# Twelve-layer decoder on one core: the eight stack-building DMAs of each 16-head self attention move from SyncE's queue to ScalarE's

## The reference, cut to what matters

```python
def heads(W):
    return (x @ W).reshape(B, S, NUM_HEADS, D_K).transpose(0, 2, 1, 3)   # 16 heads, D_K = 8
Q, K, V = (heads(WQ), heads(WK), heads(WV))
score = jnp.einsum('bhqd,bhkd->bhqk', Q, K) / jnp.sqrt(jnp.asarray(D_K, x.dtype))
score = score + mask                                   # causal
score = score - jnp.max(score, axis=-1, keepdims=True)
score = jnp.exp(score)
score = score / jnp.sum(score, axis=-1, keepdims=True)
out = jnp.einsum('bhqk,bhkd->bhqd', score, V)
```

## Time and profile before

| | |
|---|---|
| median of 3 runs | 3130.19 us (3121.03 to 3132.73) |
| the profiled execution | 3134.6 us, span 3132.9 us |
| granted TensorE clock, mean | 0.849 |
| PE busy | 2589.2 us, 83% |
| DVE busy | 1766.1 us, 56% |
| ACT busy | 1299.1 us, 41% |
| POOL busy | 635.5 us, 20% |
| DMAs `stacks<-parts` | 96 of 256 KB |

### The profile page before, as it was taken

The page is one execution under the profiler, slowest core; times in us unless marked ns, Lnnn a source line. Parts: engine busy times, 40 slices in busy tenths (PEclk is TensorE's granted clock), DMA queues, the critical chain, the costliest instruction groups (busy, mean ns, idle before and its releaser), DMA issues.

```text
span 3132.9 us, 38544 instructions
## 1 busy us (share of the span) xinstructions
PE 2589.2 (83%) x13201; PEld 1302.8 (42%) x13201; DVE 1766.1 (56%) x4879; ACT 1299.1 (41%) x3060; POOL 635.5 (20%) x893
## 2 busy tenths in 40 slices
PE   5788898789987887887758988987899888878865
PEld 2233335334544685224323333452345447742243
DVE  5544437645654688625455544486356448876164
ACT  1555621452323542574324556214532344434741
POOL 1320001320112583000113100013201137720000
PEclk7899897788877998888759988987798789988886
DMA  5100002200100001200210000022001000021000
GB/s 179 29 1 1 1 1 53 54 2 21 34 14 1 1 28 34 49 1 31 65 27 10 1 1 1 1 53 53 2 21 34 14 1 1 29 54 28 1 1 7
DMA packets 42054, 73.34 MB, mean 23 GB/s; under 512 B 2881, under 2 KB 34689, under 8 KB 40066
## 3 DMA queue, kind: packets, MB, share of 16 engines
q1 hardware_dynamic: 41282, 69.58, 8.7%
q10 hardware_dynamic: 576, 1.29, 0.1%
HBM read 43.86 MB, written 1.05 MB: 14 GB/s over the span
## 4 chain that ended last, share of the span: by engine, by line
PE 61%; DVE 18%; ACT 10%; issue 7%; DMA 2%; POOL 2%; ACTq 0%; DVEq 0%; POOLq 0%; SPq 0%
PE psum L564 4%; PE psum L986 4%; PE psum L2159 4%; PE psum L997 3%; DVE floor_s L2258 3%; PE psum L554 3%; ACT PT_s L1018 2%; PE psum L1534 2%; PE psum L810 2%; PE psum L1364 2%; PE psum L735 2%; ACT PT_s L630 2%; PE psum L1826 2%; DVE mx_s L699 2%; PE psum L537 2%
## 5 line engine op out<-in xcount | busy, mean ns | idle before, releaser
L630 ACT ACTIVATE PT_s<-psum 128x512 f32<-128x512 f32 (+3 forms) x768 | 342.5, 499 | 249.5 <-PE psum L554 247.8
L386 POOL TENSOR_SCALAR ve<-mv 128x4 f32<-128x4 f32 x48 | 13.5, 282 | 1609.1 <-DVE mv L376 1608.9
L2185 POOL TENSOR_TENSOR buffer<-sim_s 128x1024 f32<-128x1024 f32 x128 | 270.7, 2130 | 165.0 <-DVE floor_s L2258 86.9
L537 PE MATMUL psum<-stacks_s 64*128 64x512 bf16 (+3 forms) x768 | 210.7, 402 | 100.9 <-DMA stacks_s<-parts_s 39.7
L696 DVE CUSTOM_DVE_ANT_0 rest_s<-psum,packed_early 128x128 f32<-128x128 f32 (+3 forms) x512 | 225.1, 488 | 71.7 <-PE psum L537 69.2
L564 PE MATMUL psum<-PT_s,vaug 128*9 128x512 f32 (+3 forms) x1536 | 183.5, 554 | 57.3 <-POOL PT_s L669 40.1
L554 PE MATMUL psum<-stacks_s 64*128 64x512 bf16 (+3 forms) x768 | 194.5, 369 | 38.1 <-ACT PT_s L630 24.0
L669 POOL TENSOR_SCALAR_AFFINE_SELECT PT_s<-PT_s 128x128 f32<-128x128 f32 x512 | 148.1, 300 | 359.5 <-ACT PT_s L630 355.1
L2218 ACT ACTIVATE above_s<-buffer,below_s 128x1024 f32<-128x1024 f32 x128 | 145.7, 1151 | 132.2 <-PE psum L2159 88.3
L1036 ACT ACTIVATE PT_s<-psum 128x512 f32<-128x512 f32 (+1 forms) x224 | 121.2, 593 | 167.9 <-PE psum L988 167.8
L699 DVE TENSOR_REDUCE mx_s<-psum 128x1 f32<-128x512 f32 x256 | 160.1, 686 | 44.3 <-PE psum L537 43.5
(11 more groups left out here) (448 smaller groups left out, 5074.6 us busy)
## 6 DMA issues: line engine op xcount, KB each, us to landing
stacks_s<-parts_s SPq DMA_DIRECT2D x96, 256.0 KB, 5.6
buffer<-packed_experts SPq DMA_DIRECT2D x36, 384.0 KB, 3.5
buffer<-packed_moe SPq DMA_DIRECT2D x4, 2048.0 KB, 8.3
buffer<-packed_cross SPq DMA_DIRECT2D x4, 2048.0 KB, 7.5
buffer<-packed_product SPq DMA_DIRECT2D x4, 1024.0 KB, 4.7
packed_early<-packed_early SPq DMA_DIRECT2D x1, 2654.0 KB
raw_s<-packed_setup SPq DMA_DIRECT2D x1, 1840.0 KB, 6.9
packed_late<-packed_late ACTq DMA_DIRECT2D x4, 314.0 KB, 3.8
```

The lines of the kernel that those rows point to most:

```text
L537: pe.matmul(bank[n % 4][:, 0:n_keys], QS[half(h), h // 2, j * P:(j + 1) * P], KS[half(h), h // 2, 0:n_keys], start=True, stop=True, tile_p ...
L630: a.activation(PT[:, u // 4 % 2, i, q0_of(c):T], bank[u % 3][:, q0_of(c):T], ACT.Exp, scale=scale).then_inc(exp_done.sem, 1)
L2185: g.tensor_tensor(fs[:, n % 2], m[:, 0, :].unsqueeze(2).to_broadcast([P, NK, NK]), m[:, 1, :].unsqueeze(1).to_broadcast([P, NK, NK]), ALU. ...
```

## The change

The waits and the eight DMAs leave SyncE's generator and stand in ScalarE's, behind its four copies of the parts, at the same planned time `T1 - 2`. Tiles, transfers, semaphores and everything on TensorE, VectorE and GpSimd stay as they are.

```diff
     def sync(sp):
-        yield T1 - 2
-        for ready in (keys_split(4), queries_split(4), keys_repeated(2), queries_repeated(2), pads_set(3)):
-            sp.wait_ge(*ready)
-        for loaded, (first, last) in zip(pairs_loaded, PAIR_GROUPS):
-            for i in range(first, last):
-                sp.dma_start(stacks[:, :, i, :], parts[2 * HD8 * i:2 * HD8 * (i + 1)]).then_inc(loaded.sem, 16)
         for t, kind, u in plan:
             yield t
             if kind == "spread":
@@ def scalar(a): behind the four copies of the parts
                 a.copy(to, parts[:, FIRST_SLOT[name][n]:FIRST_SLOT[name][n] + 1, q, :].to_broadcast(to.shape)).then_inc(repeated.sem, 1)
+        yield T1 - 2
+        for ready in (keys_split(4), queries_split(4), keys_repeated(2), queries_repeated(2), pads_set(3)):
+            a.wait_ge(*ready)
+        for loaded, (first, last) in zip(pairs_loaded, PAIR_GROUPS):
+            for i in range(first, last):
+                a.dma_start(stacks[:, :, i, :], parts[2 * HD8 * i:2 * HD8 * (i + 1)]).then_inc(loaded.sem, 16)
         for t, kind, u in plan:
             yield t
             if kind == "rows":
```

## The result

The changed kernel is slower: median 3215.07 us (3213.81 to 3222.24, 4 runs) against 3128.11 us (3121.03 to 3132.73, 4 runs), ratio 1.0278, 95% interval 1.0260 to 1.0296, which is +87 us. Measured again on another chip, beside nine more runs of the kernel before, it was 1.0265 (1.0251 to 1.0279), +83 us. The forecast was 3210 us, +80. The profiled execution has a span of 3220.5 us where the one before had 3132.9.

The account below looks back on a forecast made before the run. No engine was taken as full: a chain of short hand-overs in fixed orders bounds the kernel. Terms 58.2 + 14.6 + 7.2 = 80.0 us on 3130.2 gave 3210 us, 3198 to 3230 with clock bounds, range 3150 to 3242.

Parts of the forecast that it names:

- The hold: At each burst, issuing the eight DMAs keeps ScalarE from starting anything for 11.6 us, as it held SyncE's queue.
- Rivals 1 and 3: Each burst holds ScalarE only 5.0 us (rival 1: 3150 us, chance 0.11) or 3.6 us (rival 3: 3141 us, 0.05).
- rival 2: Issue is slower on ScalarE: every DMA 2.12 us, 17.0 a burst, 3269 us; chance 0.04.
- Beside exponentials: Six bursts beside the other stream's exponentials: five cost 9.8 us each and the last 9.2, 58.2 us in all.
- my list of signs: What the trace would show, such as TensorE idle 10 to 11 us at the second burst with "ACT" as releaser.
- Beside the product-key feed-forward: Fifth and eleventh bursts: `above` starts later and TensorE goes on 7.3 us later each, 14.6 us in all.
- Beside the gated attention: Third and ninth bursts: a copy TensorE was waiting for starts 3.6 us later each, 7.2 us in all.
- The first and the seventh burst: Cost 0: ScalarE does nothing beside the first; the seventh's moved copy stays hidden with 0.3 us of cover.
- SyncE's relief: Part one: SyncE's queue is rid of twelve times 11.6 us, taken as worth 0.
- Rival 4: Only SyncE's relief is seen, activations going on while DMAs are issued: 3130 us or a little less; chance 0.04.
- The clock: TensorE's clock restarting at 0.50 behind each of ten bursts: bounded at -12 to +20 us, taken as 0.
- Rival 5: TensorE's clock stays low longer after each pause, at ten bursts: +25 us, 3235 us; chance 0.10.

Follow-up runs that it names:

- the spaced kernel: Against the kernel before, ScalarE issues all eight DMAs of each burst, 2.5 units of planned time apart; measured 0.9991 (0.9974 to 1.0008).
- The stream-1 kernel: Against the kernel before, only the six bursts of stream 1, those beside the other stream's exponentials, are issued by ScalarE; measured 1.0180, +56 us.
- 18 copies: Against the kernel before, DMAs stay on SyncE; ScalarE gets the waits and 18 linked copies, 11.7 us together, at each burst; measured 1.0256, +80 us.
- two DMAs: Against the kernel before, ScalarE issues the first two DMAs of each burst, SyncE the other six at the same time; measured 1.0110, +32 us.
- half the hold: Against the kernel before, all DMAs on SyncE, ScalarE gets the waits and 9 linked copies, 5.81 us, at each burst; measured 1.0049, +15 us.

## Why the prediction was right

**The hold** was forecast at 11.6 us a burst from SyncE's rows, and is 11.5 to 11.8 at eleven bursts, 10.8 at the seventh. Rivals 1 and 3 (5.0 and 3.6 us) and rival 2 (17.0) fall with it. The reason that I gave, a queue that lets the issuer on only as fast as transfers drain, is borne out by the spaced kernel.

**Beside exponentials** I had 9.8 and 9.2 and it is 9.6 to 9.7: at the second burst the exponential moved by 11.39 us instead of 11.90, because in this execution the last copy, and with it the burst, came 0.65 us earlier, and TensorE's own step differs from the sum of the two waits by some tenths. TensorE stood still for 11.8 us there, not the 10 to 11 of my list of signs. At the last burst I had 9.2 and it is 9.7. The 2.56 us of waiting were saved in full, but part was given back by the clock, which I had at 0: the four matmuls of line 570 behind the pause ran at 0.50. Before, and in the changed kernel:

```profile
2821.35 0.66 PE L570 MATMUL psum<-packed_early,qk_s 128*128 128x128 f32 x4 [0.16 <-ACT qk_s L633]
...
2913.08 1.11 PE L570 MATMUL psum<-packed_early,qk_s 128*128 128x128 f32 x4 [11.93 <-ACT qk_s L633]
```

That my 58.2 came out as 57.9 is therefore in part luck: five bursts a little under, one over. The stream-1 kernel shows the term alone, 57.1.

**Beside the product-key feed-forward** 7.3 was forecast and 7.30 and 7.25 came. TensorE of the changed kernel at the fifth burst (as the earlier trace rows):

```profile
1222.48 1.04 PE L537 MATMUL psum<-stacks_s 64*128 64x512 bf16 x4 [1.44 <-DMA stacks_s<-parts_s]
1230.79 1.97 PE L2159 MATMUL psum<-packed_early,above_s 128*128 128x128 f32 x8 [7.27 <-ACT above_s L2218]
```

Four scores, then 7.27 us of waiting for `above`: the place and the size of the step.

**Beside the gated attention** 3.6 was forecast, 3.64 and 3.55 came. **The first and the seventh burst** cost nothing to speak of (-0.22 and 0.35): at the seventh the copy of line 400 slides 5 us and stays hidden, as ScalarE and TensorE show (as the earlier trace rows):

```profile
1585.46 10.80 ACTq L619 DMA_DIRECT2D stacks_s<-parts_s  x8
1596.31 0.59 ACT L400 COPY xT<-psum 128x512 f32<-128x512 f32 x1 [11.31 <-issue]
```

```profile
1597.93 0.66 PE L2348 MATMUL psum<-packed_early,xq_s 128*128 128x128 f32 x2 [0.75 <-DVE xq_s L2305]
```

The last row's wait is VectorE's, 0.75 us as before. The copy ends at 1596.90, 1.0 us ahead of it: the burst was 0.7 us shorter than the others, which I had not foreseen. What I overlooked here is what SyncE's four loads do once they are free to start. They come with the burst and not behind it:

```profile
1585.85 0.37 SPq L304 DMA_DIRECT2D x<-in_x  x1
```

Pairs 2 to 7 then land after 10.6 to 14.3 us instead of 5.3 to 6.3. No score waited for them, so it cost nothing; with an earlier reader it would have been a cost that my sum didn't have. The step of 0.35 is the burst's own later start (TensorE waits 9.61 us for pair 0 where it was 9.26, and pair 0 lands after 4.5 us in both).

**SyncE's relief** was worth nothing, as the rows said: nothing that was waited for had been late in its queue. Rival 4 wanted activations to go on while DMAs are issued, and falls because ScalarE started none and the time is 3215. The Trainium skill's rule on balancing DMA queues ("Perfetto Trace Analysis", DMA Optimizations), as the prediction read it, gave 3130 us. The rule is for descriptor generation as the bottleneck, and the slices of these bursts are not that: spaced out, each takes 0.57 us.

**The clock** is the term that I bounded (-12 to +20) and took as 0. It is also where a single trace misleads. Stretches of 10 us that begin at about the same work just behind the fifth burst, before and then in the changed kernel (columns as the earlier trace rows, the clock ahead of the DMA share):

```profile
1200.00:1210.00 10.00, 7.90 (x50) 5.65 (x48) 8.27 (x13) 2.74 (x3) 3.82 (x2) 0.83 0.60 111
```

```profile
1233.00:1243.00 10.00, 8.33 (x36) 5.49 (x35) 6.78 (x10) 2.30 (x2) 3.82 (x2) 0.50 0.01 2
```

Behind the pause the granted clock is still at 0.50 where it had been mostly at 1.00, and the lag grows by up to 1.6 us, of which 1.1 are left at the end of the stretch. Elsewhere such amounts come back. But the kernel with only the waits moved, whose bursts cost 0.3 us, ended 16.0 us ahead of the profiled execution before, at a mean clock of 0.863 against 0.849, in the same kind of single jumps. Ends less sums over the runs that kept all matmuls in place lie between -16.3 and +7.9 us.

The pages of the profiles show what most of this rest is: the time that TensorE needs for the same 13201 matmuls. It was busy for 2589.2 us before. In the changed kernel it was busy for 5.8 us more and the rest is +7.9; in its repeat -2.1 and -3.5; with the waits alone -18.7 and -16.3; with 18 copies +7.7 and +3.2; with two DMAs -10.7 and -12. So the 8 us that the changed kernel's trace has over its steps are within what one execution differs from another by, through the clock of its working time.

The medians (+87 and +83 for steps of 79.8 and 79.0) leave 4 to 7 us that might belong to the pauses, yet the copies left nothing over, and half the hold had 11 us less than its steps. Rival 5, a clock that stays low for +25 us, is not to be seen.

That the mean clock is lower in the changed kernel (0.837 to 0.848) says little by itself, since it counts the pauses too, and nearly all of their time passes at 0.50: over the whole span TensorE stood idle at that level for 209 us before and for 299 and 296 us in the two traces after, while it worked at that level for 737 us before and for 752 and 732 after. Whether the pauses cost the few microseconds more I leave open.

## What to carry to other kernels

ScalarE was busy for only 41% of the span, and that said nothing of what a DMA burst in its queue costs: look at the first instruction behind it, at who waits for that, and take off the waits that stood there anyway. Most of the burst's issue time here was the wait for its own transfers, so spread such a burst out (0.57 us each instead of 1.52) or leave it on an engine with nothing behind it. And be wary of splitting one burst over two queues at the same moment: here it made the first transfer some 3 us late, and held the second engine as well.

## What the runs showed of the hardware

- A queue took the first two of these 256 KB SBUF-to-SBUF DMAs at 0.57 to 0.76 us each; the third of a burst took 2.0 to 2.1 and each later one mostly 1.2 to 2.0, on SyncE's queue and on ScalarE's alike (before and after), while the DMA engines were 88 to 96% busy at 150 to 195 GB/s.
- With both queues issuing, four DMAs held ScalarE 9.6 us where eight alone held it 11.7, and pair 0's landing went from 4.5 us to 7.2 to 8.0 (with two of the eight on ScalarE to 7.3, once 5.9).
- While the DMAs were being issued ScalarE started nothing at any of the 12 bursts.
- Behind each pause of ten bursts in the changed kernel TensorE's granted clock was 0.50 when it went on, and still 3 us later.
